# Delta attention: chunks solved in two halves of 4 tokens, with key products between chunks made by masked matmuls

## The reference

```python
q = silu(dwconv_causal(x @ Wq, ...));  k, v likewise        # (b, t, H, D), D = 128
a = sigmoid(x @ Wa + ba);  beta = sigmoid(x @ Wb + bb)      # a: one decay per feature of v
def step(S, t):                                             # per batch and head, k scaled by D ** -0.5
    y = einsum('bhvk,bhk->bhv', S, k_t)
    err = y - v_t
    S = a_t[..., None] * S - (b_t[..., None] * err)[..., None] * k_t[:, :, None, :]
    o = einsum('bhvk,bhk->bhv', S, q_t)
    return S, o
```

## Time and profile before

| What | us |
| --- | --- |
| median of 3 runs | 2714.83 |
| range of the runs | 2709.8 to 2717.82 |
| profiled execution, whole | 2720.65 |
| its span (first to last instruction) | 2718.9 |
| busy in the span: TensorE, VectorE, ScalarE, GpSimd | 2081.5, 1592.5, 1141.1, 1175.9 |
| first base of a chunk phase to the first state update after it (block 0, first outer chunk) | 78.8 |
| the same in its second outer chunk | 80.2 |

### The profile page before, as it was taken

One profiled execution on the slowest core, in us unless ns is written; L12 is line 12 of the kernel. 1 busy time (PEld: TensorE's weight loads), 2 busy tenths in 40 slices (PEclk: granted clock), 3 DMA queues, 4 the chain that ended last, 5 costly groups with the idle time before them and its releaser, 6 DMA issues. The chain is left out here.

```text
span 2718.9 us, 42746 instructions
## 1 busy us (share of the span) xinstructions
PE 2081.5 (77%) x15844; PEld 1636.3 (60%) x15856; DVE 1592.5 (59%) x3191; ACT 1141.1 (42%) x2723; POOL 1175.9 (43%) x996
## 2 busy tenths in 40 slices
PE   7597449978988968657896578955689656768798
PEld 5364126656566857646776567755568655546586
DVE  2223732246664339668776787766778677546533
ACT  3112311136464428434464344743446434325433
POOL 0222022210004535968339683386733877300254
PEclk9698769979998979767797677976779757789899
DMA  8422022210007023422223222232222332020340
GB/s 282 125 24 53 0 69 43 24 38 2 22 2 231 0 34 109 126 95 94 86 74 125 96 94 86 74 119 101 94 77 80 111 114 93 32 56 2 93 138 15
DMA packets 137426, 212.96 MB, mean 78 GB/s; under 512 B 61184, under 2 KB 113680, under 8 KB 132112
## 3 DMA queue, kind: packets, MB, share of 16 engines
q1 hardware_dynamic: 129072, 200.11, 23.1%
q0 software_dynamic: 8160, 10.26, 2.4%
HBM read 187.97 MB, written 22.37 MB: 77 GB/s over the span
## 5 line engine op out<-in xcount | busy, mean ns | idle before, releaser
L2088 PE MATMUL PS<-ident,XT 128*128 128x128 f32 x512 | 112.8, 402 | 258.2 <-DVE XT L2460 245.5
L2402 DVE SCALAR_TENSOR_TENSOR XT<-M_delta,CW_delta,XT 128x256 f32<-128x256 f32 x576 | 249.9, 495 | 70.2 <-ACT M_delta L2271 40.6
L2088 PEld LDWEIGHTS PS<-ident,XT 128*128 128x128 f32 x512 | 90.4, 208 | 277.6 <-DVE XT L2460 132.7
L2037 PE MATMUL PS<-XP_delta,X 128*128 128x268 f32 (+1 forms) x1024 | 241.6, 388 | 5.5 <-DMA X<-in_L_attn_b_heads 5.5
L2037 PEld LDWEIGHTS PS<-XP_delta,X 128*128 128x128 f32 x1024 | 192.7, 189 | 55.7 <-issue 11.4
L1541 PE MATMUL PS<-XP_rffn,UW_rffn 128*128 128x512 f32 x816 | 194.6, 395 | 5.5 <-POOL UW_rffn L1495 4.6
L1976 POOL TENSOR_TENSOR DD_delta<-DD_delta,A_delta 128x64 f32<-128x64 f32 (+6 forms) x224 | 169.9, 759 | 39.2 <-ACT A_delta L2359 19.5
L1541 PEld LDWEIGHTS PS<-XP_rffn,UW_rffn 128*128 128x128 f32 x816 | 155.5, 191 | 39.5 <-issue 6.8
L1273 ACT ACTIVATE PR_attn<-PS,NM_attn 128x256 f32<-128x256 f32 (+1 forms) x384 | 130.7, 448 | 103.6 <-DVE NM_attn L1343 103.6
L1495 POOL TENSOR_TENSOR UW_rffn<-W_rffn,UW_rffn 128x512 fp32r<-128x512 f32 x34 | 44.1, 1298 | 296.0 <-ACT UW_rffn L1602 296.0
L561 POOL DMA_INDIRECT sums<-XS_moe,token_moe x46 | 71.7, 1559 | 221.0 <-ACT XS_moe L661 205.8
(11 more groups left out here) (414 smaller groups left out, 5068.6 us busy)
## 6 DMA issues: line engine op xcount, KB each, us to landing
M_delta<-gram_delta SPq DMA_DIRECT2D x32, 2304.0 KB, 8.7
X<-in_L_attn_b_heads SPq DMA_DIRECT2D x64, 512.0 KB, 3.4
EW<-in_L_ffn_w SPq DMA_DIRECT2D x24, 512.0 KB, 10.0
CB_rffn<-routes_rffn SPq DMA_DIRECT2D x20, 512.0 KB, 22.4
XN<-in_L_attn_b_outs SPq DMA_DIRECT2D x16, 512.0 KB, 3.6
F_delta<-in_L_attn_b_outs SPq DMA_DIRECT2D x4, 2048.0 KB, 8.5
W_rffn<-in_L_ffn_tiles SPq DMA_DIRECT2D x4, 1536.0 KB, 11.6
slots<-pad SPq DMA_DIRECT2D x2, 2967.0 KB, 14.7
```

Of the source, the lines that this page charges most:

```text
L2037: last = nc.tensor.matmul(PS[:, 1 + i, 0:B * (WIN - halo)], WH[:, r, i, k, :], XP[:, k, :, n * BT + halo:n * BT + WIN], start=(k == 0), st ...
L2088: last = nc.tensor.transpose(PS[:, 6 + r % 2, i * P:(i + 1) * P], W[:, B * h:B * (h + 1), :], core.ident[:])
L2402: nc.vector.scalar_tensor_tensor(TMP[:, r, i], RAW[:, r, i, :, tau:tau + BT], CW[:, i, h, tau:tau + 1], TMP[:, r, i], ALU.mult, ALU.add).t ...
```

## The change

- A chunk's 8 tokens are solved as two halves of 4. M and DD keep only the pairs inside a half: 20 instead of 36. VectorE solves the first half in 3 steps (`solve`), writes it times the decays (WH4), TensorE transposes it (2 transposes), ScalarE copies it (NH4), TensorE multiplies it by the key products between the halves (GH, 8 products), and VectorE adds the result, times decays DR, to the second half (`carry`, 4 small multiplies and an add), before it solves that in 3 steps. The answers take 8 multiplies and 4 adds instead of 8 and 8.
- Between chunks, W no longer goes through 16 transposes and 64 small products. The keys are copied apart (`keys_apart`, ScalarE, 7 copies among the state copies), products of 4 lanes with one another are made once for each outer chunk (`key_products` 32, `cross_products` 96), and GpSimd masks them so that only a lane's own product is left, times -beta (`own_lanes`, `cross_lanes`). Then each earlier chunk gives one `hop`: 4 transposes, one ScalarE copy, 16 products of 32 rows. Chunk jj needs jj hops for its base. Four zero products open the accumulation.
- `turn` (16 transposes) runs once for each outer chunk. Before the last chunk ScalarE puts the W of the earlier ones in the update's order (`natural`, 4 copies for each).
- `key_rows` moves from before the chunks to behind the second chunk's hops (first outer chunk) or the last chunk's first half (second one). The four gates of a chunk move behind its hops. ScalarE scales 3 states behind each gate, up to 14, 6 or 16 of a chunk before its answer copy and 8 or 12 behind it, by `cuts`.
- The first chunk's base is now made on VectorE (multiply and subtract) instead of by GpSimd.
- ScalarE copies the even groups of states and VectorE the odd ones.
- The stage before the blocks also makes -beta by rows: 4 matmuls of 512 columns, 2 sigmoids, a store to DRAM and 6 loads in two layouts.
- Norm's small tiles become parts of one scratch tile.

Core of the diff:

```diff
-    PAIRS = C * (C + 1) // 2
+    HC = C // 2
+    PAIRS = HC * (HC + 1)
...
+            def solve(k, half):
...
+                for s in range(HC - 1):
+                    w, at = HC - 1 - s, HC * half + s
+                    x = pair(half, s) + 1
+                    c.then(nc.vector.tensor_tensor(by_h(part(w)), k[:, :, :, x:x + w],
+                                                   by_h(FK[:, :, at:at + 1].broadcast_to([P, BH, w])), ALU.mult))
+                    c.then(nc.vector.tensor_tensor(FK[:, :, at + 1:HC * (half + 1)], FK[:, :, at + 1:HC * (half + 1)], part(w), ALU.add))
...
             def chunk(n, o, jj):
...
-                for t in range(C - 1):
-                    w = C - 1 - t
...
+                solve(k, 0)
+                nc.vector.tensor_tensor(WH4.rearrange("p (n t) -> p n t", t=HC), FK[:, :, 0:HC], near, ALU.mult).then_inc(wh_d, 1)
+                if ci:
+                    dve.wait_ge(o_d, z["o_d"] + ci)
+                base(o, jj, r, 1, FQ).then_inc(base_d, 1)
+                c.then(nc.vector.tensor_tensor(near, near, HJ[:, :, jj, 1:2].broadcast_to([P, BH, HC]), ALU.mult))
+                dve.wait_ge(res_mm, z["res_mm"] + ci + 1)
+                c.then(carry(r, 0))
+                carry(r, 1).then_inc(res_d, 1)
+                c.then(nc.vector.tensor_tensor(FK[:, :, HC:], FK[:, :, HC:], carried(0), ALU.add))
+                solve(k, 1)
...
+            def first_half(n, ci):
...
+                pe.wait_ge(wh_d, z["wh_d"] + ci + 1)
+                for g in range(2):
+                    last = nc.tensor.transpose(PS[:, 7, g * P:(g + 1) * P], WH4[:, g * P:(g + 1) * P], core.ident[:])
+                last.then_inc(ht_mm, 1)
...
+                pe.wait_ge(nh_d, z["nh_d"] + ci + 1)
...
+                for g in range(2):
+                    for k in range(4):
+                        rows = slice(OC * k, OC * (k + 1))
+                        last = nc.tensor.matmul(PS[:, 1 + k, 4 * QU + g * QU:4 * QU + (g + 1) * QU], NH4[rows, g * P:(g + 1) * P],
+                                                GH[rows, jj, g * QU:(g + 1) * QU], start=True, stop=True)
+                last.then_inc(res_mm, 1)
...
+            def hop(n, o, jj, s):
...
+                if s < jj:
+                    pe.wait_ge(wdec_d, z["wdec_d"] + rests(o, jj))
+                for i in range(4):
+                    last = nc.tensor.transpose(PS[:, 6, i * P:(i + 1) * P], WNS[:, s, i * P:(i + 1) * P], core.ident[:])
+                last.then_inc(nw_mm, 1)
...
+                pe.wait_ge(nw_d, x)
+                for i in range(4):
+                    for k in range(4):
+                        rows, at = slice(OC * k, OC * (k + 1)), slice(i * QU, (i + 1) * QU)
+                        last = nc.tensor.matmul(PS[:, 1 + k, at], NEW[rows, i], GN[rows, BLOCKS.index((s, jj + 1)), at], start=jj == 0,
+                                                stop=jj == 0 or (s == jj and i == 3))
+                if s == jj:
+                    last.then_inc(rest_mm, 1)
...
-            cuts = [0, 0, 21, 42, BH]
+            cuts = [0, 14, 22, 22, 34, 40, 48, BH, BH]
...
+                        act.wait_ge(ht_mm, z["ht_mm"] + ci + 1)
+                        nc.scalar.copy(NH4, PS[:, 7, 0:BH * HC]).then_inc(nh_d, 1)
+                        if jj < NI - 1:
+                            for x in range(jj + 1):
+                                hop(n, o, jj, x)
...
+                        for r in rows:
+                            key_rows(n, o, r)
+                        at, then = cuts[2 * jj:2 * jj + 2]
+                        for h in gates:
+                            gate(n, h)
+                            decay_state(at, min(at + 3, then))
+                            at = min(at + 3, then)
+                        decay_state(at, then)
+                        if jj + 1 < NI:
+                            answer(n, ci)
+                            decay_state(then, cuts[2 * jj + 2])
...
-                    if g < NS and g % 2:
+                    if g < NS and g % 2 == 0:
                         state_copy(n, o, g)
```

More of the change, by code:

```diff
@@ L1694, in delta_attention @@
     NR = 4
-    PAIRS = C * (C + 1) // 2
-    tri = lambda s: sum(C - r for r in range(s))
+    HC = C // 2
+    PAIRS = HC * (HC + 1)
+    tri = lambda s: sum(HC - r for r in range(s))
+    pair = lambda half, s: half * PAIRS // 2 + tri(s)
+    BLOCKS = [(s, j) for s in range(NI - 1) for j in range(s + 1, NI)]
+    HOPS = len(BLOCKS)
+    hop_no = lambda jj, s: jj * (jj + 1) // 2 + s
+    QU = 2 * B * C
     outer = Stage(core, "delta")
@@ L1784, in _ @@
             last.then_inc(z_mm, 1)
+            for n in range(NH):
+                for k in range(KD):
+                    last = nc.tensor.matmul(PS[0:H, 1 + n, :], WB[:, k, :], XT[:, k, n * NB:(n + 1) * NB],
+                                            start=(k == 0), stop=(k == KD - 1))
+            last.then_inc(row_mm, 1)
         @block.scalar
@@ L2017, in _ @@
                         pool.wait_ge(wdec_d, z["wdec_d"] + rests(o, jj))
+                    queries(n, ci)
                     if ci + 1 < NC:
                         prepare(n, ci + 1)
+                    if jj == 0:
+                        for s, (first, last) in enumerate(((1, 3), (3, 5), (5, 6))):
+                            cross_lanes(n, o, s, first, last)
             heads_and_norm(NBLK)
@@ new lines, in cross_products @@
+            def cross_products(n, o, blocks):
+                for x in blocks:
+                    old, new = BLOCKS[x]
+                    cols = slice(new * C, (new + 1) * C)
+                    bank, first = (x, 0) if 0 < x < 5 else (6, x // 5 * 4 * QU)
+                    for i in range(4):
+                        for k in range(4):
+                            at = (4 * k + i) * B
+                            y = first + i * QU
+                            last = nc.tensor.matmul(PS[OC * k:OC * (k + 1), bank, y:y + QU].rearrange("p (b q t) -> p b q t", b=B, q=2),
+                                                    KC[:, old, at * C:(at + B) * C],
+                                                    KQ[:, :, o, at:at + B, cols].rearrange("p q b t -> p b q t"), start=True, stop=True)
+                last.then_inc(cn_mm, 1)
@@ L2242, in _ @@
+                    pe.wait_ge(wdec_d, z["wdec_d"] + rests(o, NI - 1))
+                    for r in range(NR):
+                        turn(n, o, r)
                     if o + 1 < NO:
@@ new lines, in _ @@
+                        if jj < NI - 1:
+                            for x in range(jj + 1):
+                                hop(n, o, jj, x)
+                        if jj == NI - 2:
+                            act.wait_ge(wdec_d, z["wdec_d"] + rests(o, jj))
+                            for x in range(jj):
+                                natural(x)
+                        for r in rows:
+                            key_rows(n, o, r)
+                        at, then = cuts[2 * jj:2 * jj + 2]
@@ L2381, in _ @@
+                        for h in gates:
+                            gate(n, h)
+                            decay_state(at, min(at + 3, then))
+                            at = min(at + 3, then)
+                        decay_state(at, then)
+                        if jj + 1 < NI:
+                            answer(n, ci)
+                            decay_state(then, cuts[2 * jj + 2])
+                    for r in range(NR):
+                        turn(n, o, r)
                     if o + 1 < NO:
+                        answer(n, NI * (o + 1) - 1)
```

429 lines of the change are left out of this document (297 added, 132 removed).

## The result

The changed kernel takes 2732.7 us (median of 7 runs, 2724.3 to 2744.9), the kernel before 2717.8 us in the same comparison: a ratio of 1.0056, 95% interval 1.0037 to 1.0074. It is slower by 0.6%, little but clear of the noise. The profiled execution took 2733.18 us (span 2731.3), 12.5 us more than that of before. Forecast was 2696 us and a faster kernel. The rival of 2738 us, "gates displace the answers", is the nearest of the cases written down.

What follows compares the result with a forecast made beforehand. GpSimd was taken to set the chunk phase's pace, VectorE 1.2 us behind; 4 x (-8 + 4 - 3.5) + 11 = -19 us from 2720.65 gave 2701.7, as median 2696 us, range 2635 to 2742.

Steps and rivals of the forecast that it cites:

- gates displace the answers: Rival: second outer chunk's gates behind the hops make answer copy and NH4 late; +23, 2738 us; chance 0.25.
- First outer chunk: Its four chunks to the first update: -7.2 us at the low clock, -12 at the high one; -8 taken per block.
- the one left out of the sum: VectorE passes with two SBUF inputs waiting for a GpSimd operation: at most some 1 us a chunk, covered by the range.
- Second outer chunk: Its four chunks to the first update, with gates behind the hops: +4 us a block taken.
- low-clock count: Second outer chunk with TensorE at 1.2 GHz: 94.9 us from first base to first update, +11 a block.
- high-clock count: Second outer chunk with TensorE at 2.4 GHz: 76.3 us from first base to first update, -8 a block.
- State copies: Second states stage: ScalarE copying even groups brings `columns` forward behind three adds; at most 3.9 us a block, -3.5 taken.
- Setup: Once, ahead of the blocks: beta by rows, its store and loads, covered by nothing; +11 us, between +8 and +14.
- no longer sets the pace: Chunk phase: GpSimd's work falls to 15.2 us a chunk, below VectorE's 16.7, and the base stops waiting for its F.
- The sum: Whole kernel: 4 x (-8 + 4 - 3.5) + 11 = -19 us.

Runs made afterwards that it cites:

- e3: Changed kernel with only ScalarE's order within a chunk changed (answer copy ahead of key rows and gates, states scaled in idle time): 2673.7 us, ratio 0.9849 to the kernel before.
- e9: Changed kernel with only the answer's copy moved ahead of key rows and the gates' sigmoids on ScalarE: 2730.0 us, ratio 1.0013 to the kernel before.
- e12: Changed kernel with states scaled where e3 scales them, the answer's copy left behind the gates: 2692.4 us, ratio 0.9901 to the kernel before.
- e10: e3 with each gate product and sigmoid cut to 4 columns (gates not computed): 2672.8 us, ratio 0.9797 to the kernel before.
- e1: Kernel before with only the state copies swapped (ScalarE even groups, VectorE odd ones): 2708.2 us, ratio 0.9953 to the kernel before.
- e6: Changed kernel with the state copies swapped back (VectorE even groups, ScalarE odd ones): 2752.9 us, ratio 1.0118 to the kernel before.
- e13: Changed kernel with the norms of all stages but the delta stage back in separate small tiles: 2735.1 us, ratio 1.0045 to the kernel before.
- e2: Changed kernel with each gate product and sigmoid cut to 4 columns, order kept (gates not computed): 2709.3 us, ratio 0.9945 to the kernel before.
- e8: e3 with the beta rows' store and loads moved into the block stage and the second outer chunk's last chunk reordered: 2648.2 us, ratio 0.9728 to the kernel before.

## Why the prediction was wrong

- **First outer chunk: the -8 was too large a gain.** Base to base it took 18.1, 18.7, 22.3 and to the add 18.0 us, where 17.0, 17.3, 23.8 and 15.9 were counted; I had named 16 to 18 us as what chunks 0 and 1 would show. A fell by 4.3 us and not by 8, 15 us in four blocks. The term at fault, by the rows of the last section, is the one left out of the sum, VectorE's passes that stand behind GpSimd (such a pass is in chunks 0, 1 and 3, which were over the count); no run takes them out, so this is read from the trace and not tested.
- **Second outer chunk: the step that failed.** The low-clock count was 94.9 us from base to add, and 93.0 were measured; chunk by chunk 16.8, 22.1, 25.4, 30.6 counted and 18.8, 21.9, 25.0, 27.4 measured. The answer's copy was counted at 24.8 us after the base of chunk 0 and began at 25.9 (1264.74 less 1238.82). I then took +4 for +11, "one third of the way up" to the high-clock count, because the mean clock was 0.66. Measured, from the last F copy, is +9.0, +9.0 and +10.2 in three blocks, at a mean clock of 0.68 to 0.69, some 22 us in all four if the last is like them. The mean clock was no weight for a blend of two whole chains: what made `carry` late stood in ScalarE's queue, where 8 scalings take 2.45 us and 12 take 3.62, and e3 took 11.7 us out of B at a clock of 0.69 to 0.71 by ScalarE's order alone. I had written that queue down myself, answer copy, 8 or 12 states and NH4 behind the gates, and the low-clock count of it was near. That it was within 2 us is in part luck: chunk 0 was 2.0 us longer than counted, with a base pass of 2.55 us beside GpSimd, the last chunk 3.2 us shorter, and chunk 0's gates took 5.0 us and not 6.51.
- **Rival "gates displace the answers"** gave 2738 us against 2732.7 measured. Its mechanism, answer copy and NH4 late in ScalarE's queue, is shown by e3, e9 and e12, with one correction: the scalings ahead of NH4 weighed more than the answer's copy, and what the gates' own time costs is open (e10). Its number is near by luck: it had A at -7.2 (measured -4.3), the state copies at -1 (measured -5 to -7) and the second outer chunk at +11 (measured +9 to +10), which cancel in part.
- **State copies** -3.5 a block: G is 5.2 us shorter in the mean, and from the add to the last F copy, which is what the sum counted, it is 7.0. At the median the swap gave 3.2 a block (e1) and cost 5.3 when undone (e6). In e1's trace three blocks gained 4.2 to 7.8 us and one, at a clock of 0.64, lost 5.2.
- **Setup** +11: 14.8, by the stage's own rows beyond my upper bound of 14. The row products took 5.6 us, inside their bounds (3.7 taken); the rest went to store, loads and their waits.
- **GpSimd** no longer sets the pace: it is busy 60.8 of 78 us. The base's wait of 4.2 us for F is gone (0.29 us, for ScalarE's F). Not all of them are, as I had predicted: once a block, in chunk 2 of the first outer chunk, the base still waits 1.2 us for it, and GpSimd's passes hold up VectorE's as said above.
- **The sum.** 4 x (-4.3) + 4 x (-5.2) + 3 x 7.5 + 3 x (-2.2) + 14.8 + 1.2 (first block ahead of M) is -6 us; the delta stage was 5.2 us longer, so some 11 us lie in the last block's second outer chunk and tail, where B's 7.5 and, by my estimate, some 4 of the last gating come together. In the prediction's terms, -19 was forecast for what measured +5 in the stage: the second outer chunk makes some 22 us of that difference, the first 15 and the setup 4, and the state copies give back 14; the rest lies between the blocks and in the tail. The other 7.3 us of the pair are within the scatter of the stages outside. That the medians still differ by 10 to 15 us, while the delta stages of the traces differ by -0.3 to +5, I can place only in part: the changed kernel's executions range from 2720 to 2755 us. A G of 33.4 us in the mean, as in e13's trace, would make such a range, but the changed kernel's own three traces have it at 27.7 to 29.4 us. Whether G is long in the longer ones is open.

## What to carry to other kernels

Put work that is ready anyway (here the state scalings) into the idle time ahead of an engine's next wait, and not between its last wait and a hand-over that another engine needs; write down for each queue what stands in front of each hand-over. If two things stand in front of one hand-over, removing one alone doesn't show their worth together. When a chain has been counted at two clocks, keep the rival at its own price instead of blending by the mean clock. A run that cuts the columns of matmuls takes away only part of their time and can change the granted clock: read both before you call the difference the price of the work.

## What the hardware showed that was not expected

In these rows VectorE's passes with two inputs in SBUF wait until a GpSimd pass that began before them is done. Changed kernel, VectorE and then GpSimd:

```profile
1132.32 0.69 DVE L2679 TENSOR_TENSOR PS<-F_delta,DC_delta 128x512 f32<-128x512 f32 x1
1136.12 2.63 DVE L2679 TENSOR_TENSOR PS<-F_delta,DC_delta 128x512 f32<-128x512 f32 x1
...
1196.57 2.79 DVE L2731 TENSOR_TENSOR X<-X,HJ_delta 128x256 f32<-128x256 f32 x1
```
```profile
1135.31 2.89 POOL L2101 TENSOR_TENSOR M_delta<-M_delta,DD_delta 128x1280 f32<-128x1280 f32 x1
...
1196.20 2.88 POOL L2122 TENSOR_TENSOR XT<-XT,AJ_delta 128x1536 f32<-128x1536 f32 x1 [11.16 <-ACT XT L2572]
```

The same pass takes 0.69 us alone and 2.63 when GpSimd's began 0.81 us before; the 256-element pass takes 0.41 us elsewhere and here 2.79, to 0.28 us after GpSimd's end. The Trainium skill ("SBUF — State Buffer", "Who interferes with whom") states that the later one blocks fully, and these rows agree. I had allowed it 1 us a chunk and left it out of the sum; these two passes took 1.9 and 2.4 us more than alone.

The stretch G has several lengths within one execution, and the granted clock goes with it (e13, second and third block, each with the 28 us ahead of it):

```profile
1516.00:1544.00 28.00, 15.45 (x170) 12.77 (x170) 22.40 (x53) 16.11 (x51) 15.97 (x14) 0.51 0.23 73
1544.00:1578.00 34.00, 31.85 (x282) 30.73 (x282) 14.44 (x13) 12.75 (x30) 9.93 (x12) 0.75 0.10 35
1859.00:1887.00 28.00, 14.58 (x170) 12.15 (x170) 23.35 (x55) 16.66 (x52) 15.91 (x15) 0.54 0.22 66
1887.00:1925.00 38.00, 36.02 (x280) 34.88 (x280) 14.15 (x13) 12.68 (x29) 10.76 (x12) 0.64 0.10 36
```

It is 28 us at 0.94 (the changed kernel's first, above), 34 at 0.75 and 38 at 0.64, with the same 280 or so matmul records: 6 or 10 us more in a block. Long ones stand in e1, e2, e8 and e9, but also in e13, which saves nothing ahead of G, so these runs don't show that a saving ahead of it brings them. What decides when the clock rises in G no run here tells.

A matmul over 4 columns took 355 ns in e2 and e10, where one over 256 took 490 to 543 ns in the changed kernel and in e3 (means over block 0's B), and the mean granted clock of B fell from 0.68 to 0.71 down to 0.53 to 0.59, with every other matmul at its place.
